# The MoE gate folded into the cross attention's products, and its score bias added by VectorE, in a post-norm decoder layer on one NeuronCore

## The reference

```python
def _layernorm(x, axis=-1, eps=1e-05):
    m = jnp.mean(x, axis=axis, keepdims=True)
    v = jnp.var(x, axis=axis, keepdims=True)
    return (x - m) / jnp.sqrt(v + eps)
...
x = _layernorm(x + self_attention(x, w_q, w_k, w_v, w_o))      # 16 heads, softmax over 1024 keys
# cross attention, one head of width 256, BETA = 1/16
q = x @ Wq + bq;  k = ctx @ Wk + bk;  v = ctx @ Wv + bv
A = softmax(BETA * (q @ k.T))                                   # 1024 x 77 per batch
x = _layernorm(x + A @ v)
# experts
gate = softmax(x @ gate_w + gate_b);  topv, topi = top_k(gate, 2);  topv = topv / topv.sum(-1)
out = sum over e of (relu(x @ w1[e] + b1[e]) @ w2[e] + b2[e]) * combine[:, e]
x = _layernorm(x + out)
```

## Time and profile before

| | |
|---|---|
| median of three runs | 1435.49 us |
| profiled execution, span from first to last instruction (the page gives no other time of it) | 1435.9 us |
| PE busy | 1400.5 us, 98% |
| DVE busy | 1076.8 us, 75% |
| ACT busy | 863.0 us, 60% |
| POOL busy | 556.4 us, 39% |
| PE on the chain that ended last | 81% |
| granted TensorE clock, mean | 0.996 |
| 690 to 715 us (one turn of the last batch): PE busy, DVE busy | 24.57, 22.84 us |

### The profile page before, as it was taken

How to read it: one execution, slowest core, us unless ns; L and a number is a source line. 1 busy time by engine, 2 the same in 40 slices (tenths; PEclk the granted TensorE clock), 3 DMA queues, 4 the chain that set the end, 5 groups by cost and what they waited for, 6 DMA issues and landing times.

```text
span 1435.9 us, 48815 instructions
## 1 busy us (share of the span) xinstructions
PE 1400.5 (98%) x18550; PEld 933.5 (65%) x18550; DVE 1076.8 (75%) x1963; ACT 863.0 (60%) x1973; POOL 556.4 (39%) x952
## 2 busy tenths in 40 slices
PE   9999999999999999999999999999999999999995
PEld 5445455544444444444444448889889999999994
DVE  6888888888888888888999955767555655555553
...
DMA packets 108799, 147.39 MB, mean 103 GB/s; under 512 B 28027, under 2 KB 80570, under 8 KB 107546
## 3 DMA queue, kind: packets, MB, share of 16 engines
...
## 4 chain that ended last, share of the span: by engine, by line
PE 81%; DVE 8%; issue 4%; POOL 3%; ACT 1%; DMA 1%; DVEq 0%; POOLq 0%; ACTq 0%
PE pa L939 15%; PE pa L1187 14%; PE pb L939 13%; PE po L1115 13%; PE pb L1201 13%; PE px L939 6%; DVE neg L1476 3%; PE px L932 2%; PE pb L932 1%; ACT w_sb L1304 1%; PE po L1046 1%; PE po L932 1%; PE px L1021 1%; PE px L993 1%; DMA space<-y_parts,y_tags 1%
## 5 line engine op out<-in xcount | busy, mean ns | idle before, releaser
L1476 DVE TENSOR_REDUCE neg<-pa 128x1 f32<-128x1024 f32 x512 | 611.4, 1213 | 76.8 <-PE pa L939 69.3
L1304 ACT ACTIVATE w_sb<-pb 128x512 f32<-128x512 f32 x996 | 590.0, 598 | 105.2 <-PE pb L939 69.7
L939 PE MATMUL pb<-w_sb 99*32 99x512 bf16 x3984 | 392.1, 380 | 3.6 <-ACT w_sb L1304 2.0
L1420 ACT ACTIVATE space<-pa,b1T_sb 128x128 f32<-128x128 f32 x568 | 154.3, 383 | 322.7 <-PE pa L1187 320.2
L939 PE MATMUL pa<-w_sb 96*32 96x512 bf16 (+1 forms) x4208 | 323.1, 380 | 6.1 <-DVE neg L1476 6.1
L1115 PE MATMUL po<-w_sb,space 128*32 128x256 f32 x4000 | 304.6, 379 | 0.0
L1187 PE MATMUL pa<-xgT,attn_t 128*128 128x128 f32 x2272 | 269.3, 276 | 2.9 <-DVE attn_t L1814 2.9
L1187 PEld LDWEIGHTS pa<-xgT,attn_t 128*128 128x128 f32 x2272 | 265.7, 192 | 8.9 <-issue 5.6
L1201 PE MATMUL pb<-w_sb,space 128*128 x1136 | 260.4, 379 | 0.0
L1201 PEld LDWEIGHTS pb<-w_sb,space 128*128 128x128 f32 x1136 | 208.8, 190 | 25.1 <-issue 0.3
L1115 PEld LDWEIGHTS po<-w_sb,space 128*32 128x32 f32 x4000 | 124.3, 111 | 98.6
...
## 6 DMA issues: line engine op xcount, KB each, us to landing
...
```

What stands on the lines that cost most here:

```text
L939: mm = pe.matmul(out[at:end], lhsT[:, at:end], rhs, start=start, stop=stop, tile_position=(0, at))
L1304: act.activation(ex_of(n)[:, half * HALF:(half + 1) * HALF], score_bank(n, half), ACT.Exp, scale=SCALE).then_inc(e_done, 1)
L1420: ins = act.activation(hT[tile % 2][:, f, :], pH[tile % 2][:, f, :], ACT.Relu, bias=g.b1_sb[:, bass.ds(e * FT + f, 1)])
L1476: dve.tensor_reduce(neg[i % 2][:, t:t + 1], pa[n % 2][:, :], AX.X, ALU.max, negate=True).then_inc(max_done, 1)
```

## The change

The gate's logits are written in another way. With z = x1 + A v, mean m and reciprocal deviation r, layer norm gives x2 = (z - m) r, so x2 W + b = r (x1 W + A (v W) - m sum(W)) + b. The part x1 W comes from eight more columns of `fold` in `score`; A (v W) from eight more columns of `cv` in `cross`; v W and sum(W) are made in the opening. VectorE puts the parts together: `add_bias` moves 85 columns from px to SBUF and adds the score bias (for which `bias` has 128 rows now), `raw_logits` adds the two parts after the cross product, and `logits`, now in step 1 of the following turn, subtracts the mean's part and multiplies by r. `turn_2`, `copy_2` and `gate` are gone, and so is the bias product in `score`. `soft` works in place in SBUF. px is free after step 5 when the bias has been added, no longer when the softmax has read it. The norms are computed where they were. The opening's list has 13 weights, with one and a half steps after each score group.

```diff
--- before.py
+++ after.py
+CG = C + NE
+DG = D + NE
...
-    WEIGHTS = [*range(KD), *range(2 * KD + 1, 2 * KD + 1 + B), *range(KD, 2 * KD + 1)]
+    KEYS, FOLDS, BIAS, VALUES = range(KD), range(KD, 2 * KD), 2 * KD, range(2 * KD + 1, 2 * KD + 1 + B)
+    VALUES_T, GATED, GATE_SUM = range(2 * KD + 1 + B, 3 * KD + 1 + B), 3 * KD + 1 + B, 3 * KD + 2 + B
+    WEIGHTS = [*KEYS, *VALUES, *VALUES_T, *FOLDS, BIAS, GATED, GATE_SUM]
     CONSTANTS = 7
-    CROSS_LOADS = 7
+    CROSS_LOADS = 8
+    CV_MADE = 1 + KD
...
-    GATE = slice(D, D + NE)
-    RANK = [slice(D + NE + i * TB * NE, D + NE + (i + 1) * TB * NE) for i in range(2)]
+    GATE = slice(C, CG)
+    VALUE_GATE = slice(D, DG)
+    RANK = [slice(DG + i * TB * NE, DG + (i + 1) * TB * NE) for i in range(2)]
...
-        fold = sb("fold", [P, B, KD, C])
-        fold_b = sb("fold_b", [P, B * C])
-        cv = sb("cv", [CP, B, D])
...
+        fold = sb("fold", [P, B, KD, CG])
+        bias = sb("bias", [P, B, CG])
+        gate_sum = sb("gate_sum", [P, NE])
+        cv = sb("cv", [CP, B, DG])
...
-            if s == 1 and before is not None:
-                return c_copied, before + 1
             if s == 2 and j is not None:
-                if ranks_step(p) is not None:
-                    return route, routed(ranks_step(p), "rank")
-                return (logits_done, before + 1) if before is not None else (added, j + 1)
+                return (route, routed(ranks_step(p), "rank")) if ranks_step(p) is not None else (added, j + 1)
             if s == 3 and b:
                 return v_done, nth(b, p // TURN % TB)
             if s >= 4 and j is not None:
-                return ((b_copied, j + 1), (soft_done, j + 1), (p_copied, j + 1), (mixed, j + 1))[s - 4]
+                return ((b_copied, j + 1), (biased, j + 1), (p_copied, j + 1), (mixed, j + 1))[s - 4]
...
+                        pool.wait_ge(norm_2_done, TB * (b + 1))
...
+                pool.wait_ge(cross_in, 16 * CROSS_LOADS)
+                for k in range(KD):
+                    pool.tensor_copy(bq_wide[:, k, :], c_bq[:, k:k + 1].to_broadcast([P, P])).then_inc(bq_made, 1)
...
+                        for k in range(KD):
+                            pool.tensor_copy(fold[:, :, k, GATE], g.gate_sb[:, k:k + 1, :].to_broadcast([P, B, NE])
+                                             ).then_inc(cv_made, 1)
+                        pool.tensor_tensor(cv[0:C, :, 0:D], cv[0:C, :, 0:D],
...
-                        if i == KD:
-                            pe.wait_ge(weights_made, KD)
+                        if i == FOLDS[0]:
+                            pe.wait_ge(weights_made, 1 + WEIGHTS.index(KEYS[-1]))
+                        if i == BIAS:
+                            pe.wait_ge(bq_made, KD)
+                        if i == GATED:
+                            pe.wait_ge(const_in, 16 * CONSTANTS)
+                            pe.wait_ge(weights_made, 1 + WEIGHTS.index(VALUES_T[-1]))
...
+                    elif i in VALUES_T:
+                        at = VALUES_T.index(i) * P
+                        mm = whole(bank[:, 0:B * C], c_w[:, 2, k, at:at + P], c_x[:, k, :], first, last)
...
+                    elif i == BIAS:
+                        mm = whole(bank[:, 0:B * C], bq_wide[:, k, :], c_k[:, k, :], first, last)
+                    elif i == GATED:
+                        for b in range(k * B // KD, (k + 1) * B // KD):
+                            for m in range(KD):
+                                mm = whole(bank[0:C, b * NE:(b + 1) * NE], c_vT[:, m, b * C:(b + 1) * C], g.gate_sb[:, m, :],
+                                           m == 0, m == KD - 1)
                     else:
+                        mm = whole(bank[:, 0:NE], g.ones[:, :], g.gate_sb[:, k, :], first, last)
...
-                    cols = slice(b * C, b * C + C)
-                    out = px[:, 0:C]
+                    if j == 0:
+                        pe.wait_ge(cv_made, CV_MADE)
                     product = quarters if j < MAIN_PROJ else whole
                     for k in range(KD):
-                        product(out, turned_b[:, k, :], fold[:, b, k, :], k == 0, False)
-                    product(out, g.ones[:, :], fold_b[:, cols], False, True).then_inc(scored, 1)
+                        mm = product(px[:, 0:CG], turned_b[:, k, :], fold[:, b, k, :], k == 0, k == KD - 1)
+                    mm.then_inc(scored, 1)
 
                 def turn_p(j):
                     pe.wait_ge(soft_done, j + 1)
...
 
                 def cross(j):
                     pe.wait_ge(p_copied, j + 1)
-                    if j == 0:
-                        pe.wait_ge(cv_made, 1)
                     product = quarters if j < MAIN_PROJ else whole
-                    product(px[:, 0:D], prT[:, :], cv[:, j // TB, :], True, True).then_inc(crossed, 1)
-
-                def turn_2(j):
-                    b, t = divmod(j, TB)
...
-
-                def gate(j):
...
-                    elif s == 1:
-                        turn_2(before)
                     elif s == 2:
                         proj(j)
-                        if before is not None:
-                            gate(before)
...
+                steps = [(m, k) for m in range(1, len(WEIGHTS)) for k in range(KD)]
                 for n in range(2 * LEAD):
                     score_max(n)
-
-                    m, k = divmod(n + KD, KD)
-                    if m < len(WEIGHTS):
+                    for m, k in steps[3 * n // 2:3 * (n + 1) // 2]:
...
-                    if MAIN_GATE <= j - 1 < NT:
-                        if j < NT:
-                            pe.wait_ge(added, j + 1)
+                    down(tile, CHUNKS[1], e)
+                    if tile == 0:
+                        last_reps()
+                    if MAIN_PROJ <= j < NT:
+                        pe.wait_ge(added, j + 1)
                         if tile == SHIFT + 1:
                             pe.wait_ge(route, routed(B - 2, "rank"))
                         if tile == 1:
                             pe.wait_ge(last_scaled, 2)
-                        turn_2(j - 1)
-                    down(tile, CHUNKS[1], e)
-                    if tile == 0:
-                        last_reps()
-                    if MAIN_PROJ <= j < NT:
-                        pe.wait_ge(c_copied, j)
                         turn_1(j)
                     down(tile, CHUNKS[2], e)
                     if MAIN_PROJ <= j < NT:
                         score(j)
-                    if MAIN_GATE <= j - 1 < NT:
-                        gate(j - 1)
...
-                def copy_2(j):
...
-
                 def soft(j):
                     t = j % TB
                     act.wait_ge(cmax_done, j + 1)
-                    if j:
-                        act.wait_ge(p_turned, j)
-                    act.activation(pr[:, 0:C], px[:, 0:C], ACT.Exp, bias=cneg[:, t:t + 1],
+                    act.activation(pr[:, 0:C], pr[:, 0:C], ACT.Exp, bias=cneg[:, t:t + 1],
...
+                def add_bias(j):
+                    dve.wait_ge(scored, j + 1)
+                    if j:
+                        dve.wait_ge(p_turned, j)
+                    dve.tensor_tensor(pr[:, 0:CG], px[:, 0:CG], bias[:, j // TB, :], ALU.add).then_inc(biased, 1)
+
                 def cross_max(j):
                     t = j % TB
-                    dve.wait_ge(scored, j + 1)
+                    dve.wait_ge(biased, j + 1)
                     if j >= TB:
                         dve.wait_ge(soft_done, j - TB + 1)
-                    dve.tensor_reduce(cneg[:, t:t + 1], px[:, 0:C], AX.X, ALU.max, negate=True).then_inc(cmax_done, 1)
+                    dve.tensor_reduce(cneg[:, t:t + 1], pr[:, 0:C], AX.X, ALU.max, negate=True).then_inc(cmax_done, 1)
...
+                def raw_logits(j):
+                    t = j % TB
+                    dve.wait_ge(crec_done, j + 1)
+                    dve.wait_ge(crossed, j + 1)
+                    dve.scalar_tensor_tensor(lg[:, t, :], px[:, VALUE_GATE], crec[:, t:t + 1], pr[:, GATE], ALU.mult, ALU.add
+                                             ).then_inc(gate_raw, 1)
...
                 def logits(j):
-                    dve.wait_ge(gated, j + 1)
-                    dve.tensor_tensor(lg[:, j % TB, :], px[:, GATE], g.gate_b_sb[:, :], ALU.add).then_inc(logits_done, 1)
+                    t = j % TB
+                    dve.wait_ge(gate_raw, j + 1)
+                    dve.wait_ge(rstd_2_done, j + 1)
+                    dve.scalar_tensor_tensor(lg[:, t, :], gate_sum[:, :], mv_b[:, t, 0:1], lg[:, t, :], ALU.mult, ALU.add
+                                             ).then_inc(gate_centred, 1)
+                    dve.wait_ge(gate_centred, j + 1)
+                    dve.scalar_tensor_tensor(lg[:, t, :], lg[:, t, :], rstd_b[:, t:t + 1], g.gate_b_sb[:, :], ALU.mult, ALU.add
+                                             ).then_inc(logits_done, 1)
...
+                    if s == 1 and before is not None:
```

(15 more changed lines are left out.)

97 lines of the change are left out of this document (47 added, 50 removed).

## The result

The changed kernel takes 1447.2 us (median of four executions, 1445.65 to 1450.99) against 1435.4 us of the kernel before beside it (1435.2 to 1435.9): 1.0082 times, with a 95% interval of 1.0068 to 1.0097. It is slower by 11.8 us, outside the range given. The profiled execution is its slowest, with a span of 1449.2 us, so 13.3 us of span are to be explained.

What follows compares the result with a forecast made beforehand. TensorE, 98% busy, was taken as bound only outside a step-5 chain through VectorE and ScalarE, with VectorE nearly binding the last batch. Opening +4.7, full turns −4.3 and smaller terms gave −1.0 us; forecast 1434.5 us, range 1421 to 1440.

Steps and rivals of the forecast that it cites:

- the last turn: Last attention turn: it has no maxima to make, so −0.3 us.
- The opening, +4.7: Opening: TensorE is busy there, so new weight products are paid; +4.7 us, between 3.5 and 6.5.
- Full turns, 14 × −0.31: Attention turns of tiles 1 to 14: TensorE's saving less the chain's growth, 0.31 us each, −4.3 us together.
- Chain growth 0.27: Step 5 of each turn: bias addition 0.24 us and hand-over 0.03 us lengthen the chain from TensorE's pa to pb.
- Outside the chain TensorE saves 0.47 + 0.12: Full turns: x2 transposes with their gap (0.47 us) and gate matmuls (0.12 us) save 0.59 us.
- Last batch, 7 × −0.1: Turns of tiles 15 to 21: VectorE sets the pace from step 6 to step 2; net −0.1 us each, −0.8 us.
- only 0.59 us at step 2: Last batch's turns: VectorE, nearly the bound, waits for TensorE only 0.59 us, at step 2.
- Expert tiles, −0.08 each: Expert tiles carrying attention tiles: a loop through all engines sets the period; −0.08 us in six regular tiles, −0.5 us.
- From norm_1's end VectorE needs ... 2.27 us; then ... bias, maximum, and the 0.79 us to the transposes of the probabilities: Expert tiles: the route from norm_1 to the probabilities' transposes takes 3.56 us where 3.71 stood, −0.15 us.
- +0.6 us forecast for three: Three expert tiles that carry routing are VectorE's already: +0.6 us together.
- VectorE's chain costs more: Rival, chance 0.20: bias addition and hand-over cost 0.5 us, deciding from about 0.35 us; +8 us, 1443.5 us.
- TensorE's saving comes through: Rival, chance 0.08: TensorE's savings in turns and expert tiles are won, less the opening's 4.7; −22 us, 1413.5 us.

Runs made afterwards that it cites:

- logits-earlier run: The changed kernel with the two logits operations and best moved in front of norm_1 in the expert tiles; ratio 1.0090 to the kernel before.
- bias-on-TensorE run: The changed kernel with the score bias back on TensorE as one more product, VectorE copying the eight gate columns; 1439.98 us, ratio 1.0027 to the kernel before.
- better version: The changed kernel with the score bias back on TensorE and the logits finished on GpSimd in the turns only; 1454.45 us beside 1457.14 us, ratio 0.9979.
- run without the gated values: The changed kernel without the opening's two products for the transposed values and eight small gate products, gate columns of the values zero; ratio 1.0034 to the kernel before.

## Why the prediction was wrong

The sum missed the profiled span by 14.3 us: 1.1 in the opening, 3.4 in the full turns, 5.4 in the last batch, 0.3 in the last turn and 4.1 in the expert tiles and behind them.

- **The opening, +4.7.** Its products cost 4.0 us, in the bounds of 3.5 to 6.5. What it missed is the granted clock, which I had read as 1.00 everywhere and taken as fixed: here 1.5 us in the profiled execution, none in some others (the logits-earlier run's trace has no fall in the opening), more in the bias-on-TensorE run, where it is below 1.00 from 51 to 59 us. With the falls at 809 and 1052 us, 0.9 us each against the same stretches before, the clock goes with about 3.3 of the 13.3 us. The late transfer has the other 1.0 us of this stretch.
- **Full turns, 14 × −0.31.** Chain growth 0.27 forecast, 0.28 measured, and gate products 0.12, right. The step that failed is "Outside the chain TensorE saves 0.47 + 0.12": with the gate left out and nothing added, a turn saves 0.47 in all, so the x2 transposes were worth about 0.35, not 0.47. The rest is TensorE's new wait for neg at 326.30. Bias alone costs 0.23 (26.69 less 26.46). It gives −0.15 a quiet turn. Two turns went the other way, tile 11's by 0.19 us and tile 12's by 0.52 us, the latter with the logits operation of 1.51 us in it; those of tiles 4 and 8, with the operations of 0.92 and 1.07 us, came out equal.
- **Last batch, 7 × −0.1.** A quiet turn: 0.40 saved (24.90 to 24.50 with bias on TensorE and logits on GpSimd), 0.20 lost by the logits on VectorE (24.70), 0.24 by the bias (24.94): +0.04, against −0.1. That term was mis-sized a little: the raw logits take 0.14 us to the next start (669.20 to 669.34) where 0.08 was forecast, the two that finish the logits 0.40 us (675.71 to 676.11) where 0.26 was. (That VectorE waits for TensorE "only 0.59 us at step 2" was read wrongly, too: in a quiet turn before it also waits 0.80, 0.74 and 0.55 us in steps 4 to 6, at 653.39, 659.65 and 662.61.) What failed is multiplying it by seven, as if all turns were the quiet one of the earlier trace rows. In the turn that ends at tile 16's x1 transposes the logits operation met GpSimd's scaling (+0.95). In those of tiles 18 and 19, +0.40 and +0.60, VectorE also does the routing, and from its wait of 0.47 us at 770.23 on it waits no more than 0.17 us up to 786.44, so the additions on that way are paid in full; tile 21's +0.52 is of this size too, and wasn't taken apart. Tile 20's +2.18 is the longer wait around the held table operation and the late transfer, 1.3 us, and the fall of the clock behind it, 0.9 us. What the turn costs depends on where VectorE's queue meets the scaling: −0.77 us with the logits in step 4.
- **Expert tiles, −0.08 each.** The step that failed is the route: "From norm_1's end VectorE needs ... 2.27 us; then ... bias, maximum, and the 0.79 us to the transposes of the probabilities". That hand-over route was no longer the last one. VectorE's own queue goes from norm_1 past the maximum through logits, best, third norm, result, reciprocal and raw logits to the mixing, and the additions on it are 0.29 for the bias, some 0.5 for the logits and 0.15 for the raw logits; from them come off what VectorE had waited, 0.30 us for the gate product and 0.31 us for the cross attention's. That leaves some 0.3 us of the 0.41 us by which the mixing is later; the rest are small differences behind it on the queue. The period is 10.99 instead of the forecast 10.54 us. The same route was forecast 0.15 us shorter and became 0.38 us shorter at the product with the values, which then waited for VectorE. The bias run (10.68) shows that the bias part of it is real, and the mixing 0.46 us sooner in the logits-earlier run that the logits part is. The two tiles with routing, +1.6 us, against +0.6 us forecast for three, weren't taken apart.
- **The rivals.** "VectorE's chain costs more" came nearest, at 1443.5 us, but for a reason that isn't its own: the pair costs 0.28 us, well under the 0.35 at which it was to decide. I let that price decide between faster and slower. What decided was how much else on VectorE had no cover. "TensorE's saving comes through" is out: without the gate the gain is 11.5 us, not 22, with nothing paid for it.
- Shown by runs: bias 7 to 8 us; the logits' place and engine in the turns (1.0027 to 0.9979 on the better version, on different chips, so some 0.5%); all of TensorE's gate work 11.5 us. Argued from rows only: the opening's products (4.0 us), the late transfer in it, tile 20, the price of the clock's falls.
- The chips differ in the expert tiles. Where the better version was timed, its period is 10.97 us, like the changed kernel's 10.99 us beside it: VectorE waits 0.72 us for the projection there instead of 0.41 us, though mixing and projection start as in the bias run (5.78 and 6.31 us behind the x1 transposes in both). On the chip where best was moved, the tiles of the kernel before take 11.24 to 11.50 us, and the changed ones (the run without the gated values) 11.05 to 11.32 us: the loss of 0.37 us a tile is not there at all. So the expert tiles' loss by the change and gain by the bias on TensorE were seen on one chip alone, and the changed kernel's 1.0043 to 1.0082 differ partly for that reason. What makes the projection late there wasn't looked for.
